# A six-layer graph attention stack in slots of one layer: row minima ahead of the join's normalise, and the mask added in the minima

## The reference

```python
# layer 0 (8 heads), x: graphs x 128 x 256
q, k, v = x @ Wq + bq, x @ Wk + bk, x @ Wv + bv
attn = softmax(where(adj == 0, -inf, q k^T * 32**-0.5))
x = layer_norm(x + (attn v) @ Wo + bo) * gamma + beta
# layer 1
x = layer_norm(x + softmax(masked(x Wq (x Wk)^T / 16)) (x Wv) @ Wo + bo) * gamma + beta
# layers 2 to 5
w = where(mask, 0, softmax(where(mask, -1e10, (x Wq^T + bq)(x Wk^T + bk)^T / sqrt(128))))
x = layer_norm(x + (w x) @ Wc^T) * ln_g + ln_b
```

## Time and profile before

| | us |
|---|---|
| median of 3 runs (2487.67 to 2492.85) | 2490.63 |
| the profiled execution | 2490.31 |
| its span, first to last instruction | 2488.5 |
| PE busy | 2363.7 (95%) |
| POOL busy | 1843.6 (74%) |
| DVE busy | 1695.1 (68%) |
| ACT busy | 1576.8 (63%) |

### The profile page before, as it was taken

One profiled execution on the slowest core, in us unless ns is written; L12 is line 12 of the kernel. 1 busy time (PEld: TensorE's weight loads), 2 busy tenths in 40 slices (PEclk: granted clock), 3 DMA queues, 4 the chain that ended last, 5 costly groups with the idle time before them and its releaser, 6 DMA issues.

```text
span 2488.5 us, 57766 instructions
## 1 busy us (share of the span) xinstructions
PE 2363.7 (95%) x21200; PEld 2179.7 (88%) x21200; DVE 1695.1 (68%) x4945; ACT 1576.8 (63%) x5515; POOL 1843.6 (74%) x2437
## 2 busy tenths in 40 slices
PE   6899999999999999999999999999999999999985
PEld 5789989989989989989889889889889889889874
DVE  4576676676776776776776776776776766766763
ACT  5576666666666666666666666666666666666642
POOL 4577777777777777777777777777777777777763
PEclk9999999999999999999999999999999999999997
DMA  3000000000000000000000000000000000000000
GB/s 145 22 25 31 19 29 31 18 29 31 18 29 27 22 29 27 21 31 27 21 31 25 22 31 22 25 31 23 25 31 23 25 31 22 25 31 12 14 9 13
DMA packets 38728, 68.66 MB, mean 28 GB/s; under 512 B 4400, under 2 KB 12848, under 8 KB 37936
## 3 DMA queue, kind: packets, MB, share of 16 engines
q1 hardware_dynamic: 38448, 64.97, 7.6%
HBM read 48.18 MB, written 16.78 MB: 26 GB/s over the span
## 4 chain that ended last, share of the span: by engine, by line
PE 65%; DVE 19%; ACT 7%; POOL 6%; issue 3%; DVEq 0%; DMA 0%; POOLq 0%; SPq 0%
PE value_bank L406 13%; PE qk_bank L398 12%; PE context_bank L559 8%; PE unit_bank L398 7%; PE qk_bank L512 5%; DVE y L868 5%; DVE y L849 4%; PE unit_bank L469 4%; POOL rstd L961 4%; ACT probs L639 4%; PE unit_bank L406 4%; DVE bn L857 3%; PE score_bank L543 3%; PE unit_bank L481 3%; PE score_bank L540 2%
## 5 line engine op out<-in xcount | busy, mean ns | idle before, releaser
L979 POOL TENSOR_TENSOR x<-y,rows 128x512 f32<-128x512 f32 x320 | 409.5, 1280 | 220.2 <-DVE y L868 218.6
L868 DVE TENSOR_SCALAR y<-y,mv,rstd 128x256 f32<-128x256 f32 x768 | 371.8, 526 | 280.9 <-POOL rstd L961 280.9
L661 ACT CAST xT_hi<-qk_bank 128x512 fp32r<-128x512 f32 x320 | 187.7, 587 | 432.1 <-PE qk_bank L512 432.1
L398 PE MATMUL qk_bank<-xT_hi,w_lo 128*128 128x256 f32 x1280 | 405.4, 317 | 53.5 <-DVE xT_lo L812 53.3
L985 POOL TENSOR_TENSOR x<-x,rows 128x512 f32<-128x512 f32 x320 | 413.4, 1292 | 25.1
L406 PE MATMUL value_bank<-w_lo,xT_hi 128*128 128x256 f32 x1280 | 393.9, 308 | 0.2 <-ACT v L679 0.2
L639 ACT ACTIVATE probs<-unit_bank,negmax 128x128 f32<-128x128 f32 x1024 | 365.5, 382 | 34.8 <-DVE negmax L779 34.8
L398 PE MATMUL qk_bank<-xT_lo,w_hi 128*128 128x256 f32 x1280 | 363.4, 284 | 0.0
L406 PE MATMUL value_bank<-w_hi,xT_lo 128*128 128x256 f32 x1280 | 361.7, 283 | 0.0
L398 PE MATMUL qk_bank<-xT_hi,w_hi 128*128 128x256 f32 x1280 | 361.2, 282 | 0.0
L406 PE MATMUL value_bank<-w_hi,xT_hi 128*128 128x256 f32 x1280 | 360.1, 281 | 0.0
(11 more groups left out here) (93 smaller groups left out, 6477.4 us busy)
## 6 DMA issues: line engine op xcount, KB each, us to landing
x0T<-xT_in SPq DMA_DIRECT2D x64, 256.0 KB, 3.0
x<-x_in SPq DMA_DIRECT2D x64, 256.0 KB, 3.0
out<-x_out SPq DMA_DIRECT2D x64, 256.0 KB, 2.2
adj<-adj_in SPq DMA_DIRECT2D x64, 128.0 KB, 2.1
late_weights<-w_in SPq DMA_DIRECT2D x2, 1024.0 KB, 7.4
rows<-rows_in SPq DMA_DIRECT2D x1, 1792.0 KB, 12.1
probs0T<-w_in SPq DMA_DIRECT2D x4, 256.0 KB, 3.9
x<-w_in SPq DMA_DIRECT2D x1, 1024.0 KB, 13.0
```

Source lines behind the costliest of these rows:

```text
L398: mm = pe.matmul(psum[:, n * G * N:(n + 1) * G * N], split(w, name, kd, at, at + P), flat(xT_half[:, kd]), start=kd == 0 and w is w_lo, st ...
L868: m = dve.tensor_scalar(y[:, r, g], y[:, r, g], mv[:, r, g, 0:1], rstd[:, r, g:g + 1], ALU.subtract, ALU.mult)
L979: pool.tensor_tensor(result(norm), y[:, NORM_AT[norm] % YS], row_of_each(f"gamma{layer}"), ALU.mult).then_inc(zg_ready, 1)
```

## The change

It has two parts. The mask of layers 1 to 5 is no longer a product on PE. `row_max` becomes two `tensor_tensor_reduce`, one a graph, that read the scores in `score_bank` and the mask in SBUF, write their sum to a new SBUF tile `scores`, and keep the minimum of each row. `softmax` reads `scores` in place of `score_bank`. The first score product of each graph now starts its own accumulation.

The second part is order. On DVE the join's `normalise` moves from the end of slot 5g-2 into slot 5g-1, behind `row_max` and `split_lo`. On POOL `scale` and `shift` of the group go ahead of the item's `shift`, and since that turns the order in which results are finished, waits on `x_ready` count by a new list `RESULTS`.

```diff
--- before.py
+++ after.py
@@ -84,6 +84,10 @@
          ([("group", due(i, 2))] if due(i, 2) is not None else [])]
 NORM_AT = {n: at for at, n in enumerate(NORMS)}
 
+RESULTS = [n for i in SLOTS for n in ([("group", due(i, 2))] if due(i, 2) is not None else []) +
+           ([("item", i - 2)] if item(i - 2) else [])]
+RESULT_AT = {n: at for at, n in enumerate(RESULTS)}
+
 
 def layer_and_group(norm):
     kind, which = norm
@@ -170,6 +174,7 @@
         qT = sb("qT", [KD, G, N])
         kT = sb("kT", [G, N])
         v = sb("v", [RING, G, D])
+        scores = sb("scores", [RING, G, N])
         probs = sb("probs", [RING, G, N])
         probsT = sb("probsT", [RING, G, N])
         SMALL = 4
@@ -347,7 +352,7 @@
                 sp.dma_start(adj[:, r], adj_in[group // S][:, group % S]).then_inc(adj_loaded[r], 16)
 
             def store(group):
-                sp.wait_ge(x_ready, NORM_AT["item", PERIOD * group + STEP * (LAYERS - 2)] + 1)
+                sp.wait_ge(x_ready, RESULT_AT["item", PERIOD * group + STEP * (LAYERS - 2)] + 1)
                 sp.dma_start(out[group // S][:, group % S], x_out[:, group % STORES]).then_inc(stored[group % STORES], 16)
 
             load_x0T(0)
@@ -504,7 +509,7 @@
 
             def transpose_x(i):
                 layer, group = item(i)
-                pe.wait_ge(x_ready, NORM_AT[source_of(i)] + 1)
+                pe.wait_ge(x_ready, RESULT_AT[source_of(i)] + 1)
                 if NTH[i] > 0:
                     pe.wait_ge(qk_ready, NTH[i])
                 for kd in range(KD):
@@ -533,15 +538,14 @@
                 pe.wait_ge(qk_ready, after(i))
                 if NTH[i] > 0:
                     pe.wait_ge(probsT_ready, NTH[i])
-                pe.matmul(score_bank[:, 0:G * N], eye16[:, :], flat(mask[:, group % HELD]), start=True, stop=False)
                 for g in range(G):
                     if layer == 1:
                         for kd in range(KD):
                             mm = pe.matmul(score_bank[:, g * N:(g + 1) * N], qT[:, kd, g], xT[:, kd, g],
-                                           start=False, stop=g == G - 1 and kd == KD - 1)
+                                           start=kd == 0, stop=kd == KD - 1)
                     else:
                         mm = pe.matmul(score_bank[:, g * N:(g + 1) * N], qT[:, 0, g], kT[:, g],
-                                       start=False, stop=g == G - 1)
+                                       start=True, stop=True)
                 mm.then_inc(scores_in_psum, 1)
 
             def transpose_probs(i):
@@ -681,7 +685,7 @@
             def softmax(i):
                 act.wait_ge(negmax_ready, after(i))
                 for g in range(G):
-                    e = act.activation(probs[:, ring(i), g], score_bank[:, g * N:(g + 1) * N], ACT.Exp, scale=-1.0,
+                    e = act.activation(probs[:, ring(i), g], scores[:, ring(i), g], ACT.Exp, scale=-1.0,
                                        bias=negmax[:, small(i), g:g + 1], accum_out=total[:, small(i), g:g + 1])
                 e.then_inc(exp_ready, 1)
 
@@ -814,8 +818,11 @@
 
             def row_max(i):
                 dve.wait_ge(scores_in_psum, after(i))
-                dve.tensor_reduce(negmax[:, small(i)], by_graph(score_bank, N), mybir.AxisListType.X,
-                                  ALU.min).then_inc(negmax_ready, 1)
+                for g in range(G):
+                    m = dve.tensor_tensor_reduce(scores[:, ring(i), g], score_bank[:, g * N:(g + 1) * N],
+                                                 mask[:, held(i), g], 1.0, LARGEST, ALU.add, ALU.min,
+                                                 negmax[:, small(i), g:g + 1])
+                m.then_inc(negmax_ready, 1)
 
             def move_v1(i):
 
@@ -888,6 +895,8 @@
                     row_max(i - 1)
                 if item(i):
                     split_lo(i)
+                if (group := due(i, 1)) is not None:
+                    normalise(("group", group))
                 if (group := due(i, 2)) is not None:
                     split_headsT(group)
                 if (group := due(i, 6)) is not None:
@@ -921,7 +930,6 @@
                 if (group := due(i, 2)) is not None:
                     add_residual(("group", group))
                     statistics(("group", group))
-                    normalise(("group", group))
                 if i == -5:
                     for n in range(2):
                         dve.wait_ge(w1_hi_ready, n + 1)
@@ -1009,11 +1017,10 @@
 
                 if (group := due(i, 2)) is not None:
                     find_rstd(("group", group))
+                    scale(("group", group))
+                    shift(("group", group))
                 if item(i - 2):
                     shift(("item", i - 2))
-                if (group := due(i, 2)) is not None:
-                    scale(("group", group))
-                    shift(("group", group))
 
 
 # ---- launch: one core; the host only lays data out ----
```

## The result

The changed kernel takes 2450.63 us (median of 4 runs, 2450.26 to 2451.63) against 2491.61 for the kernel before on the same chip. The ratio is 0.9839, with a 95% interval of 0.9822 to 0.9856.

A forecast was written before the change was run, and what follows sets the result against it. The prediction took PE, busy 95% of the span, to bound the kernel, with some starts set by DVE, POOL and ACT. 61 groups gave -2 us, start and end +2, so 2490 us; range 2465 to 2532 for 8 in 10.

The forecast's parts named there:

- R: Time from the start of DVE's new row minima to the start of its next instruction; taken as 0.62 us, between 0.52 and 0.76.
- the walk: Step-by-step timing of one group g, from its join (slot 5g-2) through slot 5g+1; ends at -0.03 us a group.
- 1, minima start: DVE at the join: scores end at 1218.01 and the row minima start at 1218.05.
- 2, `normalise` of the group: DVE, behind `split_lo`: starts at 1218.65 + R = 1219.27, takes 0.74 us, ends at 1220.01 against 1220.79 before.
- 4, scale of the group: POOL starts the group's scale at 1219.47 + R, with the group's shift and then the item's shift behind it.
- 4, next item's `var_eps`: POOL finds the next item's `rstd` only behind the item's shift, at 1223.32 + R = 1223.94, against 1224.07 before.
- 5, its `normalise`: DVE normalises the next item 1.05 us later, at 1224.37 + R = 1224.99; minima and `split_lo` queue behind it.
- 5, projection of slot 5g: PE's projection waits for DVE's `split_lo` and starts at 1227.02, against 1227.26 before.
- 6, value product: PE, behind ACT's exponentials: starts at 1227.93 + 2R = 1229.17, against 1229.15 before; nothing left of the gain.
- 7, projection of slot 5g+1: DVE's minima start at 1232.67; `xT_lo` and PE's projection come R + 0.74 later, at 1234.03 against 1233.84 before.
- The rival of cheap minima: New DVE minima cost little more than the old: R = 0.50, -0.39 us a group, -24 us, 2468 us; chance 0.27.
- 3R - 1.89: Predicted change of a group in us; breaks even at R = 0.63; some 61 groups at -0.03 give -2 us.

## Why the prediction was wrong

The prediction's place for every step was right, and one term was mis-sized. The kernel after is 18.59 us earlier on its clock than the kernel before at the item's residual in slot 5g-2, which lies ahead of the instructions that the change moves. The rows of before and after:

```profile
1212.70 0.88 DVE L849 SCALAR_TENSOR_TENSOR y<-context_bank,rtotal,x 128x256 f32<-128x256 f32 x2 [0.55 <-PE context_bank L559]
```

```profile
1194.11 0.88 DVE L856 SCALAR_TENSOR_TENSOR y<-context_bank,rtotal,x 128x256 f32<-128x256 f32 x2 [0.44 <-PE context_bank L563]
```

With that shift and R = 0.43 the walk gives, in the clock of the kernel after:

| step | predicted in letters | with R = 0.43, shifted | measured |
|---|---|---|---|
| 1, minima start | 1218.05 | 1199.46 | 1199.47 |
| 2, `normalise` of the group | 1218.65 + R | 1200.49 | 1200.54 |
| 4, scale of the group | 1219.47 + R | 1201.31 | 1201.35 |
| 4, next item's `var_eps` | 1223.32 + R | 1205.16 | 1205.19 |
| 5, its `normalise` | 1224.37 + R | 1206.21 | 1206.24 |
| 5, projection of slot 5g | 1225.78 + 2R | 1208.05 | 1208.06 |
| 6, value product | 1227.93 + 2R | 1210.20 | 1210.23 |
| 7, projection of slot 5g+1 | see below | 1214.87 | 1214.91 |

For step 7 the value product is 0.36 sooner than before by the walk, so the minima start at 1232.76 - 0.11 - 0.36 = 1232.29, and the projection R + 0.74 later at 1233.46, which is 1214.87 on the clock of the kernel after. All eight are met within 0.05 us.

**The step that failed** is the price of the new minima, R between 0.52 and 0.76, taken as 0.62. Its parts:

- *The main instruction.* I took 0.24, between 0.21 (like the old minima) and 0.27 (like the residual). Measured from start to start it is 0.21 to 0.22. The old minima were the right neighbour. What the residual costs more does not come from having two inputs, since the new instruction has two as well. The rows of before could have told: `xT_lo` has two inputs and 512 elements and takes 0.68 us, as long as a reduction of 512, which has one. The row is below. What the residual's extra 0.06 us does come from no run here shows.
- *The readout.* I took 0.07, between 0.05 (like the smallest DVE instruction) and 0.11 (like ACT's readout). It is 0.00: the next instruction starts with it and runs beside all of its 83 ns. My lower bound was no bound. It came from an instruction that reads an operand, the reciprocal; whether a readout costs nothing because it reads none, no run here shows.

```profile
1221.64 0.68 DVE L779 TENSOR_REDUCE negmax<-unit_bank 128x4 f32<-128x512 f32 x1
```

Over the two graphs these parts were 0.19 us too long together, and 61 groups take that three times: 35 of the 39 us between 2490 and the result. Most of the other 4 lie outside of the repeating middle, where I had put a loss of 2 us for longer minima. The first `score0` starts 1.05 us later than before (14.73 against 13.68), but from the last one to the end of the span it is 2.2 us less (143.4 against 145.5), so the ends give 1 us instead. Which instructions give it is open.

The low end of the range, R = 0.48, therefore stood on a wrong floor. The rival of cheap minima was the right case (I gave it 0.27), and even it was not cheap enough. The Trainium skill ("VectorE: DVE Perf Modes", The DRAIN you can't avoid) says that an operation waits for an empty pipe, and that one which isn't held starts earlier. The rows show only the second case: nothing of R waits. Its section "Two Vector instructions with no wait between them" judges the readout of an accumulator output like any other instruction, held where start quadrants differ. They are the same here, and the rows agree. The estimate by the errata table of the same page, 0.32 us a graph, is about as far from the measured 0.215 as my 0.31 was.

One smaller term was too small as well. The exponentials that read SBUF cost 0.05 together by my estimate. Before, two of them and their readouts took 1227.12 - 1226.42 = 0.70 on ACT's timeline, and after it is 0.79 (the rows at 1207.43 and 1208.22 below show it). That is 0.09 and not 0.05, of which 0.02 more than I took reaches the value product. It starts 2.80 behind them (1210.23), against 2.73 plus 0.05:

```profile
1207.43 0.40 ACT L688 ACTIVATE probs<-scores,negmax 128x128 f32<-128x128 f32 x1 [0.79 <-DVE negmax L822]
...
1208.22 0.35 ACT L643 ACTIVATE probs<-unit_bank,negmax 128x128 f32<-128x128 f32 x1
...
1209.59 0.59 ACT L683 COPY v<-value_bank 128x512 f32<-128x512 f32 x1
```

The mask product's 0.11 us did vanish from PE's queue, and the walk counts four of the five in a group. That fits the 8 us that the edit is worth in either order, a net of the products and the longer minima.

## What to carry to other kernels

In a pipeline that repeats, write the change of one period as a number of times the uncertain duration plus a constant, before choosing that duration. Here 3R - 1.89 showed that each 0.01 us of R weighs 2 us of time, and the range should have allowed for a readout that costs nothing. Look among the rows of before for an instruction that has the feature that is to be priced: `xT_lo` would have shown that a second input is free. Where an instruction is moved out of the shadow of a wait, look for what queues behind it: one addition of 1.3 us on POOL, moved out of a wait, cost 17 us against leaving it there, and put into another gap it gave 48.

## What the runs showed of the hardware

- The accumulator readout behind a DVE product-with-minimum (83 ns in the profile) costs nothing from start to start: the next instruction starts with it, at 1199.69, at 1199.90 and in the rows with a third minimum. On ACT the readout of an exponential is followed 0.09 to 0.10 us later.
- The product-with-minimum over 128 elements with one input in PSUM and one bf16 in SBUF takes 0.21 us from start to start. That is what the reduction of before (0.34 over 256) would take over 128 by an estimate from its rows, though the new one also reads a second operand and writes 128 elements.
- An exponential over 128 elements that reads SBUF takes 401 ns against 373 from PSUM before, and with its readout 0.045 us more from start to start (0.79 against 0.70 for two).
- DVE's two `TENSOR_SCALAR` of `normalise` take 0.74 us where POOL waits, and 1.68 where POOL's addition of 1.27 us runs beside them (the rows at 1191.05 and 1190.98).
